# A preactivated four-block network on one core: any of eight banks for each PSUM result, and the pools of one more image summed on TensorE

## What is computed

```
x = x + attention(gn(x))       # q from all 1024 pixels, k and v from a 2x2 strided conv + LayerNorm, 8 heads, 1x1 proj
x = x + selective_scan(gn(x))  # LayerNorm, 4 channel groups: in_proj, depthwise 3x3, scan in 4 directions, LayerNorm,
                               # gate, out_proj; channel gate by a small MLP; LayerNorm; proj
x = x + channel_attention(gn(x))  # 8 heads, 32x32 scores over the pixels
x = x + pools(gn(x))           # maxpools of 1,3,5,7,9,11,13; two neighbours per channel mixed by a score; + input
```

## Time and profile before

| | us |
|---|---|
| median of the runs | 857.36 |
| the profiled execution | 855.84 |
| its span | 853.2 |
| TensorE busy (3384 instructions) | 704.7 |
| VectorE busy | 561.6 |
| ScalarE busy | 424.3 |
| GpSimd busy | 32.8 |

### The profile page before, as it was taken

The page is one execution under the profiler, slowest core; times in us unless marked ns, Lnnn a source line. Parts: engine busy times, 40 slices in busy tenths (PEclk is TensorE's granted clock), DMA queues, the critical chain, the costliest instruction groups (busy, mean ns, idle before and its releaser), DMA issues.

```text
span 853.2 us, 9378 instructions
## 1 busy us (share of the span) xinstructions
PE 704.7 (83%) x3384; PEld 318.8 (37%) x3384; DVE 561.6 (66%) x1057; ACT 424.3 (50%) x703; POOL 32.8 (4%) x26
## 2 busy tenths in 40 slices
PE   4848986898988899999799887798597887889685
PEld 4514332243323356443333443133234452355331
DVE  3563438226829632775678888968996858876586
ACT  1202555379576557656665637576756335521211
POOL 3300002000001000000020000000200000000000
PEclk9956998799999999989889898999788669999889
DMA  7330131000131000003200000011000010000101
GB/s 265 101 93 1 50 85 58 2 1 0 51 89 54 1 2 1 1 2 85 58 1 2 1 1 2 0 56 44 0 1 1 0 50 1 0 0 1 50 0 49
DMA packets 15056, 26.87 MB, mean 31 GB/s; under 512 B 3314, under 2 KB 7058, under 8 KB 14883
## 3 DMA queue, kind: packets, MB, share of 16 engines
q1 hardware_dynamic: 11712, 22.80, 8.7%
q10 hardware_dynamic: 3298, 3.48, 1.4%
HBM read 14.09 MB, written 4.19 MB: 21 GB/s over the span
## 4 chain that ended last, share of the span: by engine, by line
PE 56%; DVE 22%; ACT 14%; issue 5%; SPq 1%; POOL 1%; DMA 0%; ACTq 0%; DVEq 0%; POOLq 0%
PE aD L1661 6%; PE aA L1680 4%; DVE NEGMAX L1071 4%; PE bA L1552 4%; PE aD L1680 4%; PE pp L1586 4%; PE bA L1694 3%; PE bA L1782 3%; PE aA L1646 2%; ACT PT L549 2%; PE aD L1552 2%; DVE PA_ L1398 2%; DVE HB L1393 2%; PE aD L1626 2%; PE aA L1573 2%
## 5 line engine op out<-in xcount | busy, mean ns | idle before, releaser
L549 ACT ACTIVATE PT<-aA 128x512 f32<-128x512 f32 x128 | 70.1, 593 | 85.0 <-PE aA L1646 84.5
L1071 DVE TENSOR_REDUCE NEGMAX<-aD 128x2 f32<-128x512 f32 x128 | 82.0, 684 | 24.3 <-PE aD L1626 23.0
L1626 PE MATMUL aD<-KST,QST 96*128 96x256 f16 x256 | 53.0, 312 | 25.6 <-DVE NEGMAX L1071 18.0
L1646 PE MATMUL aA<-QST,KST 98*128 98x512 f16 x128 | 45.3, 411 | 16.0 <-ACT PT L549 11.5
L1398 DVE TENSOR_TENSOR PA_<-HB 128x1024 f32<-128x1024 f32 x40 | 49.0, 1226 | 5.0 <-PE aD L1950 4.0
L1393 DVE TENSOR_TENSOR HB<-PA_ 128x1024 f32<-128x1024 f32 x40 | 48.9, 1221 | 0.6
L1626 PEld LDWEIGHTS aD<-KST,QST 96*128 96x128 f16 x256 | 19.5, 104 | 65.2 <-DVE NEGMAX L1071 38.7
L1680 PE MATMUL aA<-XNP,WTAP 64*64 64x512 f32 x288 | 37.2, 673 | 6.2 <-issue 5.7
L1552 PE MATMUL bA<-PS,WP 128*128 128x512 f32 x64 | 33.5, 663 | 9.8 <-DVE PS L1110 9.8
L880 POOL TENSOR_TENSOR GA<-GA,PT 128x1024 f32<-128x1024 f32 x8 | 19.1, 2408 | 560.3 <-ACT PT L577 560.3
L1950 PE MATMUL aD<-PA_,PT 128*128 128x512 f32 x56 | 31.2, 685 | 9.2 <-DVE PA_ L1398 5.2
(11 more groups left out here) (303 smaller groups left out, 1374.8 us busy)
## 6 DMA issues: line engine op xcount, KB each, us to landing
XF<-in_x SPq DMA_DIRECT2D x8, 512.0 KB, 3.8
QST<-QH SPq DMA_DIRECT2D x32, 128.0 KB, 2.7
XR<-in_x SPq DMA_DIRECT2D x4, 1024.0 KB, 4.9
out<-ACC SPq DMA_DIRECT2D x4, 1024.0 KB, 4.2
QST<-QL SPq DMA_DIRECT2D x16, 128.0 KB, 2.8
PS<-in_cw ACTq DMA_DIRECT2D x1, 1152.0 KB
WDS<-in_wds SPq DMA_DIRECT2D x1, 1024.0 KB, 7.0
WP<-in_wp SPq DMA_DIRECT2D x2, 256.0 KB, 7.3
```

The costliest lines, as they stand in the source:

```text
L549: e.activation(PROB[:, 4 * kt + j, :], SLOT[f"aA{j % 2}"][:, :], ACT.Exp)\
L1071: e.tensor_reduce(NEGMAX[:, h, 2 * j:2 * j + 2], SLOT[f"aD{j % 2}"][:, :].rearrange("p (t k) -> p t k", t=2), AX.X, ALU.max, negate=True). ...
L1626: mm = e.matmul(s[:, t * NK:(t + 1) * NK], QST[0:96, h, qt * P:(qt + 1) * P], KST[0:96, h, :], start=True, stop=True)
L1646: e.matmul(s[:, :], KST[0:98, h, kt * P:(kt + 1) * P], QST[0:98, h, hs(g % 2)], start=True, stop=True)\
```

## The change

1. `LATE` goes from 2 to 1. Image 1's pools leave stream M for stream L: TensorE adds them in 28 more matmuls, with 14 diagonal matrices from ScalarE, and VectorE's 12 additions (L1407) and ScalarE's two starts (L733) of that image go. Stream M serves image 0 alone.
2. The diagonal matrices lie in the output tile ACC and no longer in PT. Their waits for image 3's last LayerNorm (`n1_1`) and for the last sum of the image before (`acc6_1`) go; the wait for the last image's store, made once ahead of an image's pool statistics, stands for them.
3. The fixed banks go. The banks are PSB0 to PSB7, and a table per stream says for each image and step which one it takes.
4. The three orders are written anew. SyncE's and GpSimd's stay.

```diff
-LATE = 2
+LATE = 1
...
+BANKS_A = """
+4 5 6 7 0 1 2 3 4 5 6 7 0 1 2 3 4 6 7 0 1 2 3 4 5 6 7 0 1 2 3 4 6 57 0 1 2 3 - 0 4 1 6 2 3 7 5 4 1 6
...
 PE_ORDER = """
-F11 A33 F1 A3 F1 A3 F1 A8 F1 A3 F1 A6 F1 A2 F1 A7 F1 A5 F1 A4 C4 A4 C1 A4 C2 A2 F1 A7 C2 A2 B1 F1 B1
+F11 A17 F1 A30 F1 A6 F1 A9 F1 A11 F1 A1 F2 C4 F2 C1 A10 C2 A7 B1 A10 C1 A14 B2 A6 F1 C1 B1 A6 F1 B2
...
+class Banks:
+    def __init__(self, tensors, text, steps, first=0):
+        self.tensors, self.words, self.first = tensors, text.split(), first
+        labels = steps.split()
+        self.index, self.count = {x: n for n, x in enumerate(labels)}, len(labels)
+    def at(self, b, label, n=0):
+        return int(self.words[(b - self.first) * self.count + self.index[label]][n])
...
-        SLOT = {n: ctx.enter_context(nc.psum_tensor(n, [P, HALF], f32))
-                for n in ("aA0", "aA1", "aD0", "aD1", "bA0", "bA1", "pp0", "pp1")}
+        PSB = [ctx.enter_context(nc.psum_tensor(f"PSB{n}", [P, HALF], f32)) for n in range(8)]
...
+        def bank(st, b, step, n=0):
+            return PSB[BANKS[st].at(b, step, n)]
...
-        DG = PT[:, 0:2, 0:KPOOL * P].rearrange("p c (k n) -> p c k n", n=P)
+        DG = ACC[:, :, 0:KPOOL * P].rearrange("p c (k n) -> p c k n", n=P)
...
             def weights_on_diagonal(b):
                 if b == LATE:
-                    e.wait_ge(*dve_c.at(B - 1, "n1_1"))
                     e.wait_ge(mats_loaded, 16)
-                else:
-                    e.wait_ge(*pe_l.at(b - 1, "acc6_1"))
                 e.wait_ge(*dve_l.at(b, "coef"))
...
-                    s = take(b, f"aA{j % 2}", act_a, f"p{g}_{kt}_{j}")
+                    s = take("A", b, f"st{g}_{kt}_{j}", act_a, f"p{g}_{kt}_{j}")
...
                         if k == 0:
                             for half in range(2):
-                                take(b, ("aA", "aD")[cc] + str(half), act_l, f"o{cc}_{half}")
+                                take("L", b, f"acc0_{cc}", act_l, f"o{cc}_{half}", half)
```

More of the change, by code:

```diff
@@ L230, in __init__, with take @@
         self.last = {}
[L232 to L236, removed]
+    def take(self, e, bank, reader):
+        if bank in self.last:
+            e.wait_ge(*self.last[bank])
+        self.last[bank] = reader
 def program(nc, x, cols, mats, wq, wk, wv, wds, wp0, small16, w1s, ipx, ipz, cw, xpr, dtp, xb, xc, opw,
@@ L1030, in variance @@
                     e.wait_ge(*act.at(b, f"ln_m2{l}_{half}"))
-                    e.tensor_tensor(var[0:64, hs(half)], SLOT[f"{banks}{half}"][64:128, :], var[0:64, hs(half)], ALU.subtract)\
+                    e.tensor_tensor(var[0:64, hs(half)], bank(st, b, f"sums{l}_{half}")[64:128, :], var[0:64, hs(half)], ALU.subtract)\
                      .then_inc(*dve.step(f"ln_var{l}" if half else f"ln_var{l}_0"))
@@ L1326, in pool_score @@
                 e.wait_ge(*pe.at(b, "w2"))
-                e.tensor_tensor(SC[:, :], SLOT["pp1"][:, 0:2], COL[:, :, COLS.index("w2_b")], ALU.add).then_inc(*dve.step("sc0"))
+                e.tensor_tensor(SC[:, :], bank(last(b), b, "w2")[:, 0:2], COL[:, :, COLS.index("w2_b")], ALU.add)\
+                 .then_inc(*dve.step("sc0"))
                 e.wait_ge(*dve.at(b, "sc0"))
@@ L1501, in _, with take, columns @@
             e.wait_ge(mats_loaded, 16)
-            def columns(slot, at, w, name_or_tile):
+            def take(st, b, step, engine, label, n=0):
+                k = BANKS[st].at(b, step, n)
+                slots.take(e, k, engine.at(b, label))
+                return PSB[k]
+            def columns(s, at, w, name_or_tile):
                 for m in range(CC):
@@ L1568, in sums @@
                 for half in range(2):
-                    s = take(b, f"{banks}{half}", dve, f"ln_var{l}" if half else f"ln_var{l}_0")
+                    s = take(st, b, f"sums{l}_{half}", dve, f"ln_var{l}" if half else f"ln_var{l}_0")
                     for cc in range(CC):
@@ L1673, in convolve @@
                 e.wait_ge(*act_c.at(b, "xn1"))
-                banks = [take(b, ("aA", "aD")[cc] + str(gi), act_c, f"xd{cc}_{gi}_1") for gi in range(2)]
+                banks = [take("C", b, f"xd{cc}_{gi}", act_c, f"xd{cc}_{gi}_1") for gi in range(2)]
                 for n in range(TAPS):
@@ L1685, in convolve, with four_blocks @@
                 yield
-            def four_blocks(b, slots, engine, readers, w, src):
+            def four_blocks(b, step, engine, readers, w, src):
                 for half in range(2):
-                    take(b, f"{slots}{half}", engine, readers[half])
+                    take("B", b, step, engine, readers[half], half)
                 for half in range(2):
@@ L1693, in four_blocks @@
                         at, to = slice(64 * gi, 64 * gi + 64), 64 * (gi ^ half)
-                        mm = e.matmul(SLOT[f"{slots}{half}"][to:to + 64, :], w[at, at], src(at, gi, half), start=True, stop=True)
+                        mm = e.matmul(bank("B", b, step, half)[to:to + 64, :], w[at, at], src(at, gi, half), start=True, stop=True)
                 return mm
@@ L1707, in small_mlp @@
                 pe, dve, hidden = (last_steps(b)[0], last_steps(b)[2], HM3) if at else (pe_b, dve_b, HM1)
-                s = take(b, "pp0", dve, f"hm{l}")
+                st = last(b) if at else "B"
+                s = take(st, b, steps[0], dve, f"hm{l}")
                 e.wait_ge(*sources)
@@ L1713, in small_mlp @@
                 yield
-                s = take(b, "pp1", dve, "sc0" if at else "gate_in")
+                s = take(st, b, steps[1], dve, "sc0" if at else "gate_in")
                 e.wait_ge(*dve.at(b, f"hm{l}"))
@@ L1787, in channel_scores @@
             def channel_scores(b):
-                s = take(b, "bA0", dve_d, "srow")
+                s = take("D", b, "rows", dve_d, "srow")
                 e.wait_ge(*dve_d.at(b, "gram1"))
```

320 lines of the change are left out of this document (179 added, 141 removed), and 3 rows, old and new, of the table BANKS_B.

## The result

The changed kernel took 800.9 us, the median of four runs (799.6 to 803.8), against 857.3 for the kernel before: a ratio of 0.935, interval 0.932 to 0.939. It gained 56 us where 33 were forecast; the forecast of 824 us and its whole range, 806 to 858, lie above it.

The account below looks back on a forecast made before the run. Neither TensorE (busy 704.7 of 853.2 us) nor VectorE (561.6) fills the span, so idle time matters, differing by stage. A -11, B -14, C -6 and D -2 sum to -33, giving 824 us for the median, range 806 to 858.

Parts of the forecast that it names:

- C: Stage from 249 to 575 us, up to image 3's output product: -6 us, bounds -14 and +10.
- D: Stage from 575 us to the end, with image 1's pools added on TensorE: -2 us, bounds -25 and +21.
- A: Stage from 48 to 123 us, up to image 0's output product: -11 us, bounds 0 and -16.
- B: Stage from 123 to 249 us, up to image 1's output product: -14 us, bounds -21 and +5.
- The banks alone: Whole kernel, eight free banks without new orders: 7.3 us at most, since the readers set the pace.
- +8.3: Up to image 3's last weighted values: work formerly after image 3's attention comes before it, 8.3 us more for TensorE.
- +15.8 falls here: After image 3's output product: image 1's sums add 24.1 us on TensorE, 8.3 already paid earlier, leaving +15.8.
- I count half, -7.7: After image 3's output product: VectorE loses 12 additions, 15.4 us, of which half counts as gain, -7.7.
- Rival 1: All stages: the layout's gains come whole, -11, -21, -14 and -2, giving -48 and 809 us; chance 0.15.
- Rival 3: Image 1's sums wait for VectorE's windows ahead of image 3's scan block: +16.8, 874 us; chance 0.13.
- Rival 4: TensorE bursts into free banks, then stands, and its granted clock falls: +29 us in the third stage, 853 total; chance 0.10.
- Edits priced at nothing: Matrices in the output tile, and ScalarE's 14 more copies less two starts: no change counted.

Follow-up runs that it names:

- experiment 8's mended kernel: Changed kernel with image 1's pools back on VectorE, chunk 0's first window step placed as in the changed kernel: 813.7 us.
- experiment 5's kernel: Changed kernel with another table, each result in the bank free longest by its own trace: 799.7 us, 800.5 when run again.
- experiment 1: Kernel before, orders kept, with each result in whichever of eight banks has been free longest: 827.0 us.
- Experiment 3: Kernel before with only the scan and channel streams' results on any of their four banks, attention and C results on the old pairs: 840.5 us.
- experiment 9: Changed kernel with 12 of image 1's 14 sum steps shrunk, all waits kept: 803.4 us.
- experiments 7 and 8: Image 1's pools on VectorE, 12 additions cut to 4 elements each: 812.9 from 816.7 us; with chunk 0's window step put back, 802.7 from 813.7.
- experiment 10: Kernel before with its orders, any of eight banks, and image 1's pools on TensorE, sums right behind their windows: 864.4 us.
- experiment 11: Changed kernel with longest-free banks, 12 of image 1's sums each moved two steps earlier in TensorE's order: 824.6 us.
- experiments 2 and 3: Kernel before with half the streams on any of four banks, the rest on old pairs: attention, C and pool sums 843.4 us; the other half 840.5.
- experiment 13: Changed kernel with longest-free banks plus 81 products that nobody reads, in 11 of TensorE's pauses: 796.5 us.
- experiment 12: Changed kernel with image 1's pools back on VectorE (816.7 us), its diagonal matrices back in PT with the earlier waits: 817.0 us.

## Why the prediction was wrong

Taken together, from the kernel before at 856.6: the banks -29.6 (827.0); the new order on top -13.2 (813.7, experiment 8's mended kernel); image 1's pools on TensorE, in that order, -12.8 (800.9). The forecast was right that the new order gains ahead of image 3's output product. What failed is its price of the free banks, taken as next to nothing, and its account of C and D. By stage, from the span of one profiled execution each (two such executions of experiment 5's kernel differ by 4 us in B alone, so 1 or 2 us say nothing):

```
                              A      B      C      D     span
any bank (experiment 1)     -5.3   -4.3  -11.5  -10.8   -31.9
new order (8, mended)       -9.1  -11.5   -9.3  +21.2    -8.7
image 1's sums on TensorE   -1.3   -2.0   +1.5  -10.9   -12.7
all                        -15.7  -17.8  -19.3   -0.5   -53.3
```

*The banks alone: "7.3 us at most in the whole kernel" and "They are not a gain as they stand, since the reader sets the pace".* This is the step that failed first: the banks alone are worth 29.6 us. The pace of the readers is indeed unchanged, 0.68 us a maximum before and after. But I compared writer and reader of one bank only, and didn't ask what stands in TensorE's row behind the last score. Experiment 1 shows it at image 0: the weighted values start 7.7 us earlier. The 18.0 + 11.5 + 9.8 us of waits are nearer to 29.6 than my 7.3, but not as its account, since TensorE's idle time fell by only 2.2 us. I also took busy time for work: the scores were booked at 53.0 us and took 40.7 with eight banks, part of it pace and part of it clock. The prediction also reads the wait between two pairs of scores as 0.36 us, which is the longest; the others are 0.19.

*The rows of the scan and channel streams on pairs: not priced.* Experiment 3 puts them at 16.1 us, more than attention's. Of the waits for readers in the earlier trace rows only the 9.8 us of the last product belong to them, so the rows of waits didn't bound this gain.

*A and B: -11 and -14, measured -15.7 and -17.8.* Right in direction and inside their bounds, but 5.3 and 4.3 us of them are the banks' alone, and A's term had 1.8 for that. The exponentials did not collide with the conv's evictions, for which I had halved B's term: image 1's first eight end at 147.9 us in the changed kernel and the conv's evictions begin at 154.1.

*C: -6, measured -19.3, outside its bound of -14.* The failed step is the +8.3 for "work that came after image 3's attention now comes before it", charged in full. The stage ran 306 us with 286.4 busy instead of 326 with 289.9, with more work in it. Experiment 1's C is already 11.5 us shorter by banks alone: the 36.1 us of idle time was no measure of the room, as part of the busy time was room too (39.6 us of it at half clock, by the estimate from the trace).

*D: -2, measured -0.5.* The agreement is luck: errors of up to 21 us cancel. "+15.8 falls here" for the sums: experiment 9 prices their work at nothing. "I count half, -7.7" for VectorE's additions: they are worth 11.0 (experiments 7 and 8). The banks, at nothing here, bring 10.8. Against these stands a loss that I had not listed: the new order alone, with image 1's pools still on VectorE, makes the stage from image 3's first output product to the end 21.2 us longer (267.1 in experiment 1, 288.3 in experiment 8's mended kernel). The loss is measured; its cause is argued here and not tried. More of image 2's scan block is left over when the stage begins, since image 2's last scan residual comes 27.5 us behind image 3's product in the old order and 46.5 in the new (45.8 in the changed kernel). So the new order gains 29.9 us ahead of that product and gives 21.2 back behind it. The -2.8 for image 3's conv behind a sum came: its first half takes 7.96 us and no longer 10.65. The -6.8 for the bias columns and spread rows was not tried by itself.

*Rival 1, "All of the layout comes true", 809 us, at 0.15.* It was the closest in time, and still too slow. Its A to C, -46, met -52.8, of which 21.1 are the banks' alone and not the layout's.

*Rival 3, the sums in front of image 3's scan block.* It did not happen here, and it is real: 37.4 us in experiment 10, 24.9 in experiment 11. Its condition in the prediction, sums "between nearly every two steps", was met by the changed kernel too, so that was not the sign to look at. The sign is whether a window is ready when its sum is reached: in the changed kernel no wait of a sum for a widened window (L1458) is longer than 0.9 us, against 4.2 in experiment 10 and 6.8 in experiment 11.

*Rival 4, the clock.* The gain was not lost to it. The granted clock over the span rose from 0.895 to 0.929, to 0.910 in experiment 1 with free banks alone. The Trainium skill ("TensorE: Matmul & The Clock Gate", section "A second HAM failure mode: psum-queue depth-cycling") tells of a kernel that cycles through the banks, pauses briefly between its groups and loses throughput as its clock goes down and up. These runs don't show such a loss: with eight banks in turn the clock was higher than on pairs, and with four it was unchanged (0.896, experiments 2 and 3). The same 30 us of image 0's attention in windows, on pairs (the kernel before):

```profile
48.00:78.00 30.00, 21.77 (x77) 5.62 (x76) 21.00 (x40) 4.85 (x10) 0.00 (x0) 0.52 0.12 40
```

and on eight banks (experiment 1), at 0.71:

```profile
48.00:78.00 30.00, 19.46 (x89) 12.09 (x88) 19.21 (x39) 5.50 (x12) 0.00 (x0) 0.71 0.11 39
```

The clock is not simply low where TensorE is idle: the line with eight banks has less busy time and the higher clock, and in the first 48 us of the kernel before TensorE is idle for 18.5 us at 0.95. In the timelines above it rose after a stretch of work without a pause. What to make of it needs care: experiment 13 raised it from 0.935 to 0.966 and won 3 to 6 us.

*Edits priced at nothing.* The matrices' place was nothing (experiment 12).

## What to carry to other kernels

When a producer alternates over two buffers, price the buffers by what stands behind the producer's last write, not by the pace of writer and reader: here the readers kept their 0.68 us and the kernel gained 29.6. An order and its buffers are one choice: the changed kernel ran 56 us under the kernel before on free banks and, with attention held to its pairs, 39 us over it. Look behind the place where an order gains, too: 29.9 us won ahead of image 3's output product cost 21.2 behind it. Work moved onto an in-order engine costs by its place and readiness rather than by its length: taking the sums' work out won nothing, drawing them two steps earlier cost 25 us, and moving the pools onto TensorE gave 13 us in the new order and cost 37 in the old one. And an experiment can hide a price: beside one wait of 3.55 us, the 15.4 us of additions seemed worth 3.8 us, and 11.0 once it was gone.

## What was not expected of the hardware

Taking some 20 us of full-clock products out of one stage left its length as it was and lowered the granted clock there from 0.94 to 0.87 (experiment 9); putting 81 idle products into pauses raised it over the span from 0.935 to 0.966 (experiment 13). A short block behind a pause of 4.6 us ran at 1.98 us, behind idle products at 1.09, at a granted clock of 0.50 and 1.00.
